# Mixture of experts in a fused kernel: spreading the token weights in groups of four row tiles, and scaling a quarter of the blocks on ScalarE and GpSimd

## The chip, the cores and the metric

The kernel runs on one core of a Trainium2 chip. The metric is the device time of one execution in microseconds (us). The kernel before took 2416.99 us, the median of three runs (2410.0 to 2425.56).

## What is computed

An image of 256x256 positions with 64 channels goes through two convolution-like blocks, a recurrent scan and, last, a mixture of experts. Only the last stage is touched by the change:

```python
def _L1_ffn_ref(x, router_w, router_b, expert_w, expert_b):
    B, N, D, C, E, K = (8, 4096, 64, 64, 8, 2)
    router_probs = jax.nn.softmax(x @ router_w + router_b, axis=-1)
    top_p, top_i = jax.lax.top_k(router_probs, K)
    top_p = top_p / jnp.sum(top_p, axis=-1, keepdims=True)
    expert_out = jnp.einsum('bnd,edc->bnec', x, expert_w) + expert_b
    gathered = jnp.take_along_axis(expert_out, top_i[..., None], axis=2)
    return jnp.einsum('bnk,bnkc->bnc', top_p, gathered)
...
x = _from_tokens(t, x)              # t = tokens of x; the layer norm of t goes into the experts
x = x + _from_tokens(_L1_ffn_ref(_ln_t(t), ...), x)
```

Each token gets the sum of its two best experts, weighed by a softmax over these two. The kernel does it densely: it multiplies the token by its weight for each of the eight experts (six of them are zero) and adds all eight products.

## The kernel before

The stage is the function `experts` (from L1354). Its work is cut into 64 units of 4 rows of the image: 8 token tiles of 128 (H = 2 halves of a row, R = 4 rows). The stage is a software pipeline written out by hand: every engine runs its own list `step(s)` for s from -12 to 65 (L1478, L1567, L1648, L1727, L1827), and each part of a step works on another unit, s + 10, s + 8, s, s - 1 and so on. 48 of the steps, from s = 2, are the body of a loop of eight; the others are written out. Within an engine the order is the program's; between engines there are semaphores. Where a part depends on s modulo 4 it is called a turn below: the routing is done for four units at a time.

What a step does, with the names used later:

- VectorE: `measure(s + 10)` takes the layer norm's statistics (L1495, L1499). `choose` ranks the experts, in four parts, two in turn 0 and two in turn 1. `split_shares` (L1540, turn 3) cuts the weights into two float16 parts. `scale_inputs(s, ...)` (L1551) writes xe, the token block times its weight for each expert: 8 blocks of 128x512 in a unit, each one instruction that reads one PSUM bank of weights. `finish(s - 2)` (L1562) adds the residual.
- GpSimd: `find_scales(s + 10)` (L1603, L1606, L1608) finds the norm's scale after `measure`; `weigh` has four parts, the last of which (turn 2, L1638 to L1643) makes the weights `shares`.
- ScalarE: `take(s + 8)` (L1685) copies the turned tokens out of PSUM, `normalise(s + 9)` (L1674) is eight small activations, `store(s - 2)` issues a DMA, `weigh(s + 2)` (turn 2, L1702, L1703) makes two sigmoids for the experts' shares, `take_outputs(s - 1)` (L1719) copies the experts' sum out of PSUM, `take_logits(s + 8)` (L1693) the router's. `take_shares` (L1711) comes first in turn 3.
- TensorE: `flip(s + 8)` (L1752) is four transposes, `rate(s + 8)` (L1765) the router's matmuls, `turn_shares` (L1775, turn 3) four transposes, `turn_outputs(s - 1)` (L1822) four transposes. `add_experts(s - 1, half)` (L1810) is eight matmuls of 512 columns that add the experts into po, in two halves. `spread_out(u, p)` (L1793) brings the weights of a token tile from 32 rows of wt16 to all 128 partitions, with a 0/1 matrix `select`. It uses a 32-row strip of TensorE for each, and p is 0 to 3.

The part p of `spread_out` fills two of the four PSUM banks pb with eight matmuls from two row strips, p and p + 1. Even parts use banks 0 and 1, odd parts 2 and 3, and VectorE works on one pair while TensorE fills the other: a wait for `xe_dve` at 2p - 2 blocks guards it (L1787). `add_experts(u, 0)` waits for all eight blocks of its unit (L1803).

Of the kernel before, what the change touches and what calls it, by code (L numbers as in the profile page):

```python
# [21 lines left out]
P = 128  # L22
# [1331 lines left out]
def experts(nc, tag, x, packed, selector, out, ident, numbers):  # L1354
# [4 lines left out]
    with Scope(nc, tag) as m:  # L1359
# [11 lines left out]
        xn = [m.sb(f"xn{q}", [P, R, H, C]) for q in range(2)]  # L1371
        xt = [m.sb(f"xt{q}", [P, R * P]) for q in range(4)]
        xd = [m.sb(f"xd{q}", [P, H, R * P]) for q in range(8)]
        xe = [m.sb(f"xe{q}", [P, EP, H, R * P]) for q in range(2)]
        yt = m.sb("yt", [P, R * P])
        stats = [m.sb(f"stats{q}", [P, T, 3]) for q in range(2)]
# [23 lines left out]
        with nc.Block() as block:  # L1400
# [26 lines left out]
            m.sem(n) for n in ("counted", "var_made", "scaled", "multiplied", "known", "xn_made", "xt_made", "zt_made", "l_made", "l_copied"))  # L1427
        ranked, weighed, share_made, w_made, w_turned, w_copied, w_split = (
            m.sem(n) for n in ("ranked", "weighed", "share_made", "w_made", "w_turned", "w_copied", "w_split"))
        spread_a, spread_b, xe_dve = (  # L1430
            m.sem(n) for n in ("spread_a", "spread_b", "xe_dve"))
        e_made, y_copied, y_turned, out_made, seen = (
            m.sem(n) for n in ("e_made", "y_copied", "y_turned", "out_made", "seen"))
        RANK_STEPS, WEIGH_STEPS = 8, 6
        DVE_BLOCKS = 8
        FIRST, LAST, HEAD, TAIL = -12, G + 1, 14, 16

        def run(eng, step):
# [8 lines left out]
        with nc.Block() as block:  # L1447

            @block.sync
            def _(sp):  # L1450
                def load(u):
                    if not u.real:
                        return
                    if (u - 4).real:
                        sp.wait_ge(xn_made, u.n - 3)
                    sp.dma_start(xs[u.mod(4)][:], x[:, :, row_block(u), :]).then_inc(x_in[u.mod(4)], 16)

                def load_rest(u):
                    if not u.real:
                        return  # L1460
                    if (u - 4).real:
                        sp.wait_ge(stored[u.mod(4)], u.div(4) * 16)
                    sp.dma_start(rest[u.mod(4)][:], x[:, :, row_block(u), :]).then_inc(rest_in[u.mod(4)], 16)

                def double(u):
                    if not u.real:
                        return
                    sp.wait_ge(zt_made, u.n + 1)
                    if (u - 8).real:
                        sp.sem_inc(seen, 1)  # L1470
                        sp.wait_ge(xe_dve, (u.n - 7) * DVE_BLOCKS)
                        sp.sem_inc(seen, 1)
# [12 lines left out]
            @block.vector  # L1485
            def _(dve):
# [55 lines left out]
                def scale_inputs(u, p, h):  # L1542
                    if not u.real:
                        return
                    i = (p + h) % R
                    if p == 0 and h == 0:
# [3 lines left out]
                    dve.wait_ge(spread_b if h else spread_a, u.n * R + p + 1)  # L1550
                    dve.tensor_tensor(xe[u.mod(2)][:, :, h, i * P:(i + 1) * P],  # L1551
                                      pb[2 * (p % 2) + h][:].rearrange("p (e t) -> p e t", e=EP),
                                      xd[u.mod(8)][:, h, i * P:(i + 1) * P].unsqueeze(1).to_broadcast([P, EP, P]),
                                      ALU.mult).then_inc(xe_dve, 1)

# [11 lines left out]
                def step(s):  # L1567
                    turn = s.mod(4)
                    four = s + 4 - turn
                    scale_inputs(s, 0, 0)  # L1570
                    scale_inputs(s, 0, 1)
                    finish(s - 2)
                    scale_inputs(s, 1, 0)
                    scale_inputs(s, 1, 1)
                    measure(s + 10)
                    if turn == 0:
                        choose(four, 0)
                    if turn == 1:
                        choose(four, 2)
                    if turn == 3:  # L1580
                        split_shares(s + 1)
                    scale_inputs(s, 2, 0)
                    scale_inputs(s, 2, 1)
                    scale_inputs(s, 3, 0)
                    scale_inputs(s, 3, 1)
                    if turn == 0:
                        choose(four, 1)
                    if turn == 1:
                        choose(four, 3)
# [4 lines left out]
            def _(pool):  # L1594
# [50 lines left out]
                def twofold(t):  # L1645
                    return t[:].rearrange("p (q h) e -> p q (h e)", h=H).unsqueeze(2).to_broadcast([P, 4 * R, 2, H * E])

                def step(s):  # L1648
                    turn = s.mod(4)
                    four = s + 4 - turn  # L1650
                    if turn == 1:
                        weigh(four, 1)
                    find_scales(s + 10)
                    if turn == 0:
                        weigh(four, 0)
                    if turn == 1:
                        weigh(four, 2)
                    if turn == 2:
                        weigh(four, 3)
                run(pool, step)  # L1660

            @block.scalar
            def _(act):
# [23 lines left out]
                def take_logits(u):  # L1687
# [3 lines left out]
                    if (u - 8).real:  # L1691
                        act.wait_ge(w_made, u.div(4) - 1)
                    act.activation(logit[(u.base // 4) % 2][:, u.mod(4), :], rt[:, 0:T * E], ACT.Copy  # L1693
                                   ).then_inc(l_copied, 1)

                def weigh(u):
# [29 lines left out]

                def step(s):  # L1727
                    turn = s.mod(4)
                    if turn == 3:
                        take_shares(s + 1)  # L1730
                    take(s + 8)
                    normalise(s + 9)
                    store(s - 2)
# [10 lines left out]
            def _(pe):  # L1744
# [34 lines left out]
                def spread_out(u, p):  # L1779

                    if not u.real:
                        return
                    if p == 0:
                        pe.wait_ge(w_split, u.div(4) + 1)
                        pe.sem_inc(seen, 1)
                    if p >= 2 or (u - 1).real:
                        pe.wait_ge(xe_dve, u.n * DVE_BLOCKS + 2 * p - 2)  # L1787
                        pe.sem_inc(seen, 1)
                    rows = wt16[(u.base // 4) % 2][:, u.mod(4) * P:(u.mod(4) + 1) * P]
                    for e in range(EP):  # L1790
                        for h in range(H):
                            q = (p + h) % R
                            ins = pe.matmul(pb[2 * (p % 2) + h][:, e * P:(e + 1) * P],  # L1793
                                            select[32 * q:32 * q + 32, h, e, :], rows[32 * q:32 * q + 32, :],
                                            start=True, stop=True)
                            if e == EP - 1:
                                ins.then_inc(spread_b if h else spread_a, 1)

                def add_experts(u, half):
                    if not u.real:  # L1800
                        return
                    if half == 0:
                        pe.wait_ge(xe_dve, (u.n + 1) * DVE_BLOCKS)  # L1803
                        pe.sem_inc(seen, 1)
# [22 lines left out]
                def step(s):  # L1827
                    if s.mod(4) == 3:
                        turn_shares(s + 1)
                    spread_out(s, 2)  # L1830
                    flip(s + 8)
                    add_experts(s - 1, 0)
                    spread_out(s, 3)
                    add_experts(s - 1, 1)
                    spread_out(s + 1, 0)
                    rate(s + 8)
                    spread_out(s + 1, 1)
                    turn_outputs(s - 1)

                run(pe, step)  # L1840

# [108 lines left out]
```

## Time and profile before

| | us |
|---|---|
| median of 3 runs | 2416.99 |
| the profiled execution | 2419.92 |
| its span | 2418.2 |
| the experts' stage, from its first matmuls to the end | about 1846 to 2418 |
| of it the even part, in which every step has all its parts | about 1895 to 2345 |

The span is the time from the first instruction to the last in the profile; the profiled execution is 2.9 us above the median. All engines work in the experts' stage at once, so the time of a step (one of 64 units) is what counts: it is the distance at which a part comes again.

### The profile page before, as it was taken

Reading aid. Unit: us, or ns where it says so; the run is one execution under the profiler, and the core shown is the slowest. Engines: PE = TensorE matmul, PEld = TensorE weight load, DVE = VectorE, ACT = ScalarE, POOL = GpSimd, SP = SyncE. Lnnn points to the kernel's source line nnn. Section 1 sums busy time; section 2 is a strip of 40 time slices with the busy share of each in tenths; the row PEclk is TensorE's granted clock in tenths of the full one; section 3 lists DMA queues with packets and bytes.
Section 4 is the critical chain, followed back from the end, with each engine's and each line's share of the span. In section 5 each row is a group of like instructions: output and inputs, shape, how many; then the busy total and the mean of one; then the engine's idle time right before and its main releaser. Section 6 shows DMA issues by size and latency. Waiting matters only on the chain. (4 is left out here: it accounts for less than half of the span.)

```text
span 2418.2 us, 46313 instructions
## 1 busy us (share of the span) xinstructions
PE 1806.8 (75%) x11740; PEld 1177.9 (49%) x11740; DVE 1522.4 (63%) x4493; ACT 1138.0 (47%) x2610; POOL 1296.9 (54%) x1722
## 2 busy tenths in 40 slices
PE   5777737787746659747777764777864899999998
PEld 2444426777622238624333334777853444444443
DVE  5666512665757768736555640455673788988887
ACT  5778723333215549725555561333314555555541
POOL 6989912776857740036767660466684434433430
PEclk9999979999879989968999987999976799998999
DMA  3656545887743314956777754778864555555552
GB/s 113 184 150 182 160 110 178 292 283 256 235 136 93 94 52 90 190 162 203 219 207 216 228 150 124 231 263 281 263 200 150 152 153 159 160 151 155 156 145 74
DMA packets 508245, 423.17 MB, mean 175 GB/s; under 512 B 224690, under 2 KB 437938, under 8 KB 508082
## 3 DMA queue, kind: packets, MB, share of 16 engines
q1 hardware_dynamic: 435378, 303.87, 45.0%
q10 hardware_dynamic: 72704, 117.47, 14.3%
q8 instruction: 61, 1.00, 0.2%
q14 instruction: 102, 0.84, 0.1%
HBM read 236.68 MB, written 150.99 MB: 160 GB/s over the span
## 5 line engine op out<-in xcount | busy, mean ns | idle before, releaser
L712 PE MATMUL cp_pv<-cp_weight,cp_zt 64*128 64x320 f32 x2048 | 402.5, 493 | 144.5 <-DVE cp_b_stage L530 107.6
L843 PE MATMUL cc_sum<-a_res,cc_bch 128*128 (+1 forms) x2048 | 307.0, 299 | 89.4 <-DMA cc_bch<-b_scratch 87.7
L257 POOL TENSOR_TENSOR cc_ln_rstd<-cc_ln_var,numbers 128x8 f32<-128x8 f32 x128 | 258.2, 2018 | 202.5 <-DVE cc_ln_var L248 192.4
L528 DVE TENSOR_TENSOR a_res<-cp_pv,cp_sig 128x128 f32 (+1 forms) x512 | 191.6, 374 | 266.8 <-ACT cp_sig L659 256.8
L1551 DVE TENSOR_TENSOR ex_xe<-ex_spread,ex_xd 128x512 f32<-128x512 f32 x512 | 322.6, 681 | 36.4 <-PE ex_spread L1793 35.9
L659 ACT ACTIVATE cp_sig<-cp_pv 128x384 f32<-128x384 f32 x512 | 244.7, 491 | 199.9 <-DMA gate_scratch<-cp_sig 135.5
L843 PEld LDWEIGHTS cc_sum<-a_res,cc_bch 128*128 128x128 f32 x2048 | 273.8, 206 | 116.2 <-issue 102.7
L712 PEld LDWEIGHTS cp_pv<-cp_weight,cp_zt 64*128 64x128 f32 x2048 | 186.6, 197 | 291.1 <-issue 270.7
L933 ACT ACTIVATE cc_p<-cc_sum 128x512 f32 (+1 forms) x128 | 135.5, 1058 | 403.6 <-PE cc_sum L843 349.3
L1810 PE MATMUL ex_po<-ex_xe,ex_expert 128*64 128x512 f32 x1024 | 267.6, 646 | 0.3
L1603 POOL TENSOR_TENSOR ex_rstd<-ex_var,numbers 128x8 f32<-128x8 f32 x64 | 104.7, 1636 | 273.5 <-DVE ex_var L1499 268.1
L911 POOL TENSOR_TENSOR cc_p<-cc_p,cc_g 128x512 f32 (+1 forms) x128 | 161.9, 1265 | 130.0 <-DVE cc_g L892 114.3
L639 ACT ACTIVATE cp_xn<-cp_x,cp_lift,cp_rstd 128x64 f32<-128x64 f32 x512 | 196.7, 440 | 67.2 <-POOL cp_lift L579 67.1
L892 DVE TENSOR_TENSOR cc_g<-cc_po,cc_g 128x512 f32<-128x512 f32 x128 | 88.2, 689 | 181.2 <-PE cc_po L861 165.6
L242 DVE BATCH_NORM_STATS2 cc_ln_stats<-cc_p 128x6 f32 (+1 forms) x512 | 111.9, 281 | 141.4 <-ACT cc_p L933 141.2
L1674 ACT ACTIVATE ex_xn<-ex_x,ex_lift,ex_rstd 128x64 f32<-128x64 f32 x512 | 175.8, 428 | 20.9 <-POOL ex_lift L1608 20.9
L604 POOL TENSOR_TENSOR a_res<-a_res,cp_mask 128x512 f32<-128x512 f32 (+1 forms) x128 | 133.4, 1042 | 93.5 <-DVE cp_b_stage L530 92.0
L257 POOL TENSOR_TENSOR si_ln_rstd<-si_ln_var,numbers 128x8 f32<-128x8 f32 x64 | 127.9, 1998 | 68.0 <-DVE si_ln_var L248 68.0
L861 PEld LDWEIGHTS cc_po<-cc_weight,cc_pt 128*128 128x128 f32 x1024 | 150.0, 211 | 5.6
L613 POOL TENSOR_TENSOR cp_b_stage<-cp_b_stage,cp_mask 128x256 f32<-128x256 f32 x256 | 151.4, 613 | 0.0
L861 PE MATMUL cc_po<-cc_weight,cc_pt 128*128 128x128 f32 x1024 | 149.8, 294 | 0.0
L938 ACT ACTIVATE cc_pt<-cc_tp 128x512 f32<-128x512 f32 x128 | 77.6, 606 | 140.1 <-PE cc_tp L851 128.8
(187 smaller groups left out, 3154.0 us busy)
## 6 DMA issues: line engine op xcount, KB each, us to landing
cc_bch<-b_scratch SPq DMA_DIRECT2D x256, 256.0 KB, 4.3
gate_scratch<-cp_sig SPq DMA_DIRECT2D x128, 256.0 KB, 3.0
b_scratch<-cp_b_stage SPq DMA_DIRECT2D x128, 256.0 KB, 3.8
cc_g<-gate_scratch ACTq DMA_DIRECT2D x128, 256.0 KB, 4.1
after_conv<-cc_p ACTq DMA_DIRECT2D x128, 256.0 KB, 3.6
ex_xd<-ex_xt SPq DMA_DIRECT2D x256, 128.0 KB, 2.5
cp_x<-in_x SPq DMA_DIRECT2D x64, 256.0 KB, 3.1
cc_p<-in_x ACTq DMA_DIRECT2D x64, 256.0 KB, 3.2
```

The costliest lines, as they stand in the source:

```text
L257: pool.tensor_tensor(rstd[q][:], var[q][:], numbers[:, 0:1].to_broadcast([P, tiles]), ALU.pow).then_inc(scaled if shifts else known, 1)
L528: dve.tensor_tensor(a_res[:, :, :, bass.ds(row, 1)].rearrange("p h c i -> p h (c i)"), bank[:, :, 3 * C:4 * C], sig[u.mod(2)][:, 0, :, i, ...
L613: ins = pool.tensor_tensor(at, at, over(mask_sb[:, h, row_block(u)], CH).unsqueeze(1) .to_broadcast([P, CHUNKS, R, CH]), ALU.mult)
L639: ins = act.activation(xn[u.mod(2)][:, i, 0, :], xs[u.mod(8)][:, 0, i, :], ACT.Identity, scale=rstd[q][:, k, i * H:i * H + 1], bias=lift[q ...
L659: act.activation(sig[u.mod(2)][:, :, :, i, :].rearrange("p k h c -> p h k c"), pv[slot(u, i)][:, :, 0:3 * C].rearrange("p h (k c) -> p h k ...
L712: pe.matmul(pv[slot(u, i)][:, h, 0:COLS], zt[u.mod(2)][half, i * P:(i + 1) * P], weight[half, :], start=True, stop=True).then_inc(v_made, 1)
L843: ins = pe.matmul(psum[q][:, at:at + TI], bch[buf][:, k, :, c], a_res[:, k, bass.ds(s * SC + j * CH + c, 1), ih * TI:(ih + 1) * TI], start ...
L861: ins = pe.matmul(po[q][:, j * 2 * C:(j + 1) * 2 * C], pt[:, j * P:(j + 1) * P], weight[:], start=False, stop=True, skip_group_check=True)
L911: pool.tensor_tensor(at, at, gs[q][:], ALU.add).then_inc(added, 1)
L1551: dve.tensor_tensor(xe[u.mod(2)][:, :, h, i * P:(i + 1) * P], pb[2 * (p % 2) + h][:].rearrange("p (e t) -> p e t", e=EP), xd[u.mod(8)][:, ...
L1674: ins = act.activation(xn[q][:, i, h, :], xs[u.mod(4)][:, h, i, :], ACT.Identity, scale=rstd[q][:, t:t + 1], bias=lift[q][:, t:t + 1])
L1810: ins = pe.matmul(po[h * HALF:(h + 1) * HALF, :], expert[:, e, :], xe[u.mod(2)][:, e, h, :], start=e == 0, stop=e == EP - 1)
```

## The change

Six things are changed, all in `experts`.

1. The weights are spread in two groups of a unit, g = 0 and 1, in place of four parts. A group is 16 matmuls from all four row strips, one strip to each of the four banks.
2. A group may start only when VectorE has scaled the three blocks of the group before it and ScalarE has copied its fourth.
3. VectorE scales three of the four blocks of a group (6 of 8 in a unit).
4. ScalarE copies the fourth bank to a new buffer xw in SBUF (`take_spread`), once as the first thing of its step, and once behind `normalise`.
5. GpSimd multiplies this copy into xe (a new `scale_inputs`), once ahead of `find_scales` and once as the last thing of its step.
6. TensorE's step is put in another order, and `add_experts(u, 0)` and SyncE's `double` wait for GpSimd's two blocks as well.

```diff
+        xw = [m.sb(f"xw{q}", [P, EP, P]) for q in range(2)]
...
+        DVE_BLOCKS, POOL_BLOCKS = 6, 2
+        FOURS = [[(0, 0), (1, 1), (0, 2), (1, 3)], [(1, 0), (0, 1), (1, 2), (0, 3)]]
...
 # sync, double(u)
                         sp.wait_ge(xe_dve, (u.n - 7) * DVE_BLOCKS)
+                        sp.wait_ge(xe_pool, (u.n - 7) * POOL_BLOCKS)
...
 # vector, scale_inputs(u, g, k)
+                    dve.wait_ge(spread_made[k], u.n * 2 + g + 1)
                     dve.tensor_tensor(xe[u.mod(2)][:, :, h, i * P:(i + 1) * P],
+                                      pb[k][:].rearrange("p (e t) -> p e t", e=EP),
...
 # vector, step(s)
-                    scale_inputs(s, 0, 0)
-                    scale_inputs(s, 0, 1)
+                    for k in range(3):
+                        scale_inputs(s, 0, k)
                     finish(s - 2)
-                    scale_inputs(s, 1, 0)
-                    scale_inputs(s, 1, 1)
                     measure(s + 10)
...
-                    scale_inputs(s, 2, 0)
-                    scale_inputs(s, 2, 1)
-                    scale_inputs(s, 3, 0)
-                    scale_inputs(s, 3, 1)
+                    for k in range(3):
+                        scale_inputs(s, 1, k)
...
 # gpsimd
+                def scale_inputs(u, g):
+                    h, i = FOURS[g][3]
+                    pool.wait_ge(xw_made, u.n * POOL_BLOCKS + g + 1)
+                    pool.tensor_tensor(xe[u.mod(2)][:, :, h, i * P:(i + 1) * P], xw[g][:],
+                                       xd[u.mod(8)][:, h, i * P:(i + 1) * P].unsqueeze(1).to_broadcast([P, EP, P]),
+                                       ALU.mult).then_inc(xe_pool, 1)
...
 # scalar
+                def take_spread(u, g):
+                    act.wait_ge(spread_made[3], u.n * 2 + g + 1)
+                    if (u - 1).real:
+                        act.wait_ge(xe_pool, u.n * POOL_BLOCKS + g - 1)
+                    act.activation(xw[g][:].rearrange("p e t -> p (e t)"), pb[3][:], ACT.Copy).then_inc(xw_made, 1)
...
 # tensor, spread_out(u, g)
-                    if p >= 2 or (u - 1).real:
-                        pe.wait_ge(xe_dve, u.n * DVE_BLOCKS + 2 * p - 2)
+                    if g or (u - 1).real:
+                        pe.wait_ge(xe_dve, u.n * DVE_BLOCKS + g * 3)
+                        pe.wait_ge(xw_made, u.n * POOL_BLOCKS + g)
...
 # tensor, add_experts(u, 0)
                         pe.wait_ge(xe_dve, (u.n + 1) * DVE_BLOCKS)
+                        pe.wait_ge(xe_pool, (u.n + 1) * POOL_BLOCKS)
```

The order of three engines in the loop is shown below; in these lists a line number is that of the kernel the list belongs to. TensorE before, one step in the even part (ex_po is `add_experts`, ex_tp `flip`, ex_routing `rate`, ex_tb `turn_outputs`, ex_spread `spread_out`):

```order
L1793 MATMUL ex_spread<-ex_wt,ex_select 128x128 x8
L1752 MATMUL ex_tp<-ident,ex_xn 128x128 x4
L1810 MATMUL ex_po<-ex_xe,ex_expert 64x512 x4
L1793 MATMUL ex_spread<-ex_wt,ex_select 128x128 x8
L1810 MATMUL ex_po<-ex_xe,ex_expert 64x512 x4
L1793 MATMUL ex_spread<-ex_wt,ex_select 128x128 x8
L1765 MATMUL ex_routing<-ex_router,ex_xt 128x16 x4
L1793 MATMUL ex_spread<-ex_wt,ex_select 128x128 x8
L1822 MATMUL ex_tb<-ident,ex_yt 128x128 x4
```

And TensorE now, one step, with the start of the next:

```order
L1838 MATMUL ex_po<-ex_xe,ex_expert 64x512 x4
L1778 MATMUL ex_tp<-ident,ex_xn 128x128 x4
L1820 MATMUL ex_spread<-ex_wt,ex_select 128x128 x16
L1838 MATMUL ex_po<-ex_xe,ex_expert 64x512 x4
L1791 MATMUL ex_routing<-ex_router,ex_xt 128x16 x4
L1850 MATMUL ex_tb<-ident,ex_yt 128x128 x4
L1820 MATMUL ex_spread<-ex_wt,ex_select 128x128 x16
L1838 MATMUL ex_po<-ex_xe,ex_expert 64x512 x4
```

The transposes ex_tp (`flip`) stood ahead of the first half of ex_po and now stand behind it; the four parts of the spread have become two.

ScalarE now, one step in turn 2 (ex_xt is `take`, ex_xn `normalise`, ex_share the two sigmoids, ex_yt `take_outputs`, ex_logit `take_logits`):

```order
L1718 ACTIVATE ex_xw<-ex_spread 128x512
L1701 ACTIVATE ex_xt<-ex_tp 128x512
L1690 ACTIVATE ex_xn<-ex_x,ex_lift,ex_rstd 128x64 x8
L1718 ACTIVATE ex_xw<-ex_spread 128x512
L1749 DMA out<-ex_rest 256x1x256
L1726 ACTIVATE ex_share<-ex_gap 128x32
L1727 ACTIVATE ex_share<-ex_gap 128x32
L1743 ACTIVATE ex_yt<-ex_po 128x512
L1709 ACTIVATE ex_logit<-ex_routing 128x64
```

The two rows ex_xw are new, and the rest stands as before. GpSimd now, the same step (ex_rstd and ex_lift are `find_scales`, the next three `weigh`'s last part):

```order
L1657 TENSOR_TENSOR ex_xe<-ex_xw,ex_xd 128x4x128
L1603 TENSOR_TENSOR ex_rstd<-ex_var,numbers 128x8
L1606 TENSOR_TENSOR ex_lift<-ex_stats,ex_rstd 128x8
L1608 TENSOR_TENSOR ex_lift<-numbers,ex_lift 128x8
L1638 TENSOR_TENSOR ex_first<-ex_first,ex_share 128x256
L1639 TENSOR_TENSOR ex_second<-ex_second,ex_share 128x256
L1643 TENSOR_TENSOR ex_shares<-ex_first,ex_second 128x512
L1657 TENSOR_TENSOR ex_xe<-ex_xw,ex_xd 128x4x128
```

The first and the last row are new; between them is what GpSimd did in this step before.

## Rows read from the trace of the kernel before

**Rows 1.** Windows: busy us (x instructions) of PE, PEld, DVE, ACT, POOL; clock.

```profile
1895.00:2345.00 450.00, 422.17 (x3465) 210.06 (x3466) 394.39 (x865) 230.18 (x631) 174.86 (x251) 0.93 0.55 154
2345.00:2412.00 67.00, 60.13 (x522) 25.95 (x518) 54.96 (x94) 9.38 (x21) 7.67 (x10) 1.00 0.30 88
```

**Rows 2.** Waits, 1895 to 2345 us: us in total, times, longest us.

```profile
ACT ex_xt L1685 <- PE ex_tp L1752: 102.1, 54, 3.6
ACT ex_yt L1719 <- PE ex_po L1810: 60.6, 53, 3.2
DVE ex_xe L1551 <- PE ex_spread L1793: 27.6, 37, 1.6
PE ex_spread L1793 <- DVE ex_xe L1551: 21.7, 19, 1.3
```

**Rows 3.** Groups by line and shape, 2000 to 2200 us.

```profile
L1551 DVE TENSOR_TENSOR ex_xe<-ex_spread,ex_xd 128x512 f32<-128x512 f32 x192 | 121.1, 681 | 11.8 <-PE ex_spread L1793 11.7
```

**Rows 4.** Timeline of TensorE: one step without a wait.

```profile
2047.80 0.40 PE L1793 MATMUL ex_spread<-ex_wt,ex_select 32*128 32x128 f16 x8
2048.12 0.65 PE L1752 MATMUL ex_tp<-ident,ex_xn 128*128 128x128 f32 x4
2048.71 1.94 PE L1810 MATMUL ex_po<-ex_xe,ex_expert 128*64 128x512 f32 x8
2050.58 0.40 PE L1793 MATMUL ex_spread<-ex_wt,ex_select 32*128 32x128 f16 x8
...
2055.01 0.40 PE L1793 MATMUL ex_spread<-ex_wt,ex_select 32*128 32x128 f16 x8
```

**Rows 5.** Timeline, two steps from `flip` to ScalarE's part, then GpSimd's `weigh`.

```profile
2063.92 0.66 PE L1752 MATMUL ex_tp<-ident,ex_xn 128*128 128x128 f32 x4
...
2064.61 0.60 ACT L1685 ACTIVATE ex_xt<-ex_tp 128x512 f32<-128x512 f32 x1 [2.97 <-PE ex_tp L1752]
...
2073.08 0.43 ACT L1674 ACTIVATE ex_xn<-ex_x,ex_lift,ex_rstd 128x64 f32<-128x64 f32 x1
...
2075.73 0.22 ACT L1702 ACTIVATE ex_share<-ex_gap 128x32 f32<-128x32 f32 x1
2075.85 0.22 ACT L1703 ACTIVATE ex_share<-ex_gap 128x32 f32<-128x32 f32 x1
...
2076.45 0.63 POOL L1638 TENSOR_TENSOR ex_first<-ex_first,ex_share 128x256 f32<-128x256 f32 x1
...
2077.74 1.27 POOL L1643 TENSOR_TENSOR ex_shares<-ex_first,ex_second 128x512 f32<-128x512 f32 x1
```

**Rows 6.** GpSimd's product of two SBUF tiles of 128x512, another stage.

```profile
L911 POOL TENSOR_TENSOR cc_p<-cc_p,cc_g 128x512 f32 x96 | 121.4, 1265 | 83.9 <-DVE cc_g L892 73.6 <-DMA cc_p<-after_scan 6.7 <-DMA cc_p<-in_x 3.4
```

**Rows 7.** Timeline of TensorE: a step with a wait, then the clock falls.

```profile
2096.66 0.61 PE L1793 MATMUL ex_spread<-ex_wt,ex_select 32*128 32x128 f16 x8 [1.29 <-DVE ex_xe L1551]
2097.20 1.12 PE L1752 MATMUL ex_tp<-ident,ex_xn 128*128 128x128 f32 x4
2098.25 2.77 PE L1810 MATMUL ex_po<-ex_xe,ex_expert 128*64 128x512 f32 x8
2100.95 0.40 PE L1793 MATMUL ex_spread<-ex_wt,ex_select 32*128 32x128 f16 x8
```

**Rows 8.** Windows of TensorE: us, busy, granted clock; after two waits, and before the even part.

```profile
2097.00:2098.00 1.00, 1.00 (x10) 0.50 0.63 141
2061.00:2064.00 3.00, 1.71 (x25) 1.00 0.84 225
1846.00:1896.00 50.00, 33.35 (x176) 0.50 0.56 163
```

**Rows 9.** Timeline of TensorE and ScalarE in the last steps.

```profile
2374.85 0.62 PE L1793 MATMUL ex_spread<-ex_wt,ex_select 32*128 32x128 f16 x16
...
2377.27 1.94 PE L1810 MATMUL ex_po<-ex_xe,ex_expert 128*64 128x512 f32 x8
...
2383.83 1.51 PE L1810 MATMUL ex_po<-ex_xe,ex_expert 128*64 128x512 f32 x6
```

More of the change, by code:

```diff
@@ L1429, in experts @@
             m.sem(n) for n in ("ranked", "weighed", "share_made", "w_made", "w_turned", "w_copied", "w_split"))
-        spread_a, spread_b, xe_dve = (
-            m.sem(n) for n in ("spread_a", "spread_b", "xe_dve"))
+        spread_made = [m.sem(f"spread_made{q}") for q in range(4)]
+        xw_made, xe_dve, xe_pool = (m.sem(n) for n in ("xw_made", "xe_dve", "xe_pool"))
         e_made, y_copied, y_turned, out_made, seen = (
@@ L1434, in experts @@
         RANK_STEPS, WEIGH_STEPS = 8, 6
-        DVE_BLOCKS = 8
+        DVE_BLOCKS, POOL_BLOCKS = 6, 2
+        FOURS = [[(0, 0), (1, 1), (0, 2), (1, 3)], [(1, 0), (0, 1), (1, 2), (0, 3)]]
         FIRST, LAST, HEAD, TAIL = -12, G + 1, 14, 16
@@ L1471, in double @@
                         sp.wait_ge(xe_dve, (u.n - 7) * DVE_BLOCKS)
+                        sp.sem_inc(seen, 1)
+                        sp.wait_ge(xe_pool, (u.n - 7) * POOL_BLOCKS)
                         sp.sem_inc(seen, 1)
@@ L1540, in split_shares, with scale_inputs @@
                     dve.tensor_tensor(wt16[(u.base // 4) % 2][:], rt[:], low16[:], ALU.subtract).then_inc(w_split, 1)
-                def scale_inputs(u, p, h):
+                def scale_inputs(u, g, k):
                     if not u.real:
                         return
-                    i = (p + h) % R
-                    if p == 0 and h == 0:
+                    h, i = FOURS[g][k]
+                    if g == 0 and k == 0:
                         dve.wait_ge(doubled[u.mod(8)], u.div(8) * (16 * H * 2) + 16 * H * 2)
@@ L1549, in scale_inputs @@
                             dve.wait_ge(e_made, (u.n - 1) * H)
-                    dve.wait_ge(spread_b if h else spread_a, u.n * R + p + 1)
+                    dve.wait_ge(spread_made[k], u.n * 2 + g + 1)
                     dve.tensor_tensor(xe[u.mod(2)][:, :, h, i * P:(i + 1) * P],
-                                      pb[2 * (p % 2) + h][:].rearrange("p (e t) -> p e t", e=EP),
+                                      pb[k][:].rearrange("p (e t) -> p e t", e=EP),
                                       xd[u.mod(8)][:, h, i * P:(i + 1) * P].unsqueeze(1).to_broadcast([P, EP, P]),
@@ L1646, in twofold @@
                     return t[:].rearrange("p (q h) e -> p q (h e)", h=H).unsqueeze(2).to_broadcast([P, 4 * R, 2, H * E])
+                def scale_inputs(u, g):
+                    if not u.real:
+                        return
+                    h, i = FOURS[g][3]
+                    if g == 0:
+                        pool.wait_ge(doubled[u.mod(8)], u.div(8) * (16 * H * 2) + 16 * H * 2)
+                        if (u - 2).real:
+                            pool.wait_ge(e_made, (u.n - 1) * H)
+                    pool.wait_ge(xw_made, u.n * POOL_BLOCKS + g + 1)
+                    pool.tensor_tensor(xe[u.mod(2)][:, :, h, i * P:(i + 1) * P], xw[g][:],
+                                       xd[u.mod(8)][:, h, i * P:(i + 1) * P].unsqueeze(1).to_broadcast([P, EP, P]),
+                                       ALU.mult).then_inc(xe_pool, 1)
                 def step(s):
@@ L1652, in step @@
                         weigh(four, 1)
+                    scale_inputs(s, 0)
                     find_scales(s + 10)
@@ L1659, in step @@
                         weigh(four, 3)
+                    scale_inputs(s, 1)
                 run(pool, step)
@@ L1694, in take_logits @@
                                    ).then_inc(l_copied, 1)
+                def take_spread(u, g):
+                    if not u.real:
+                        return
+                    act.wait_ge(spread_made[3], u.n * 2 + g + 1)
+                    if (u - 1).real:
+                        act.wait_ge(xe_pool, u.n * POOL_BLOCKS + g - 1)
+                    act.activation(xw[g][:].rearrange("p e t -> p (e t)"), pb[3][:], ACT.Copy).then_inc(xw_made, 1)
                 def weigh(u):
@@ L1728, in step @@
                     turn = s.mod(4)
+                    take_spread(s, 0)
                     if turn == 3:
@@ L1732, in step @@
                     normalise(s + 9)
+                    take_spread(s, 1)
                     store(s - 2)
@@ L1777, in turn_shares, with spread_out @@
                     ins.then_inc(w_turned, 1)
-                def spread_out(u, p):
+                def spread_out(u, g):
                     if not u.real:
                         return
-                    if p == 0:
+                    if g == 0:
                         pe.wait_ge(w_split, u.div(4) + 1)
                         pe.sem_inc(seen, 1)
-                    if p >= 2 or (u - 1).real:
-                        pe.wait_ge(xe_dve, u.n * DVE_BLOCKS + 2 * p - 2)
+                    if g or (u - 1).real:
+                        pe.wait_ge(xe_dve, u.n * DVE_BLOCKS + g * 3)
+                        pe.sem_inc(seen, 1)
+                        pe.wait_ge(xw_made, u.n * POOL_BLOCKS + g)
                         pe.sem_inc(seen, 1)
@@ L1790, in spread_out @@
                     for e in range(EP):
[L1791 to L1795, printed above, removed]
+                        for k, (h, i) in enumerate(FOURS[g]):
+                            ins = pe.matmul(pb[k][:, e * P:(e + 1) * P], select[32 * i:32 * i + 32, h, e, :],
+                                            rows[32 * i:32 * i + 32, :], start=True, stop=True)
                             if e == EP - 1:
-                                ins.then_inc(spread_b if h else spread_a, 1)
+                                ins.then_inc(spread_made[k], 1)
                 def add_experts(u, half):
@@ L1803, in add_experts @@
                         pe.wait_ge(xe_dve, (u.n + 1) * DVE_BLOCKS)
+                        pe.sem_inc(seen, 1)
+                        pe.wait_ge(xe_pool, (u.n + 1) * POOL_BLOCKS)
                         pe.sem_inc(seen, 1)
@@ L1829, in step @@
                         turn_shares(s + 1)
-                    spread_out(s, 2)
+                    add_experts(s - 1, 0)
                     flip(s + 8)
-                    add_experts(s - 1, 0)
-                    spread_out(s, 3)
+                    spread_out(s, 1)
                     add_experts(s - 1, 1)
+                    rate(s + 8)
+                    turn_outputs(s - 1)
                     spread_out(s + 1, 0)
-                    rate(s + 8)
-                    spread_out(s + 1, 1)
-                    turn_outputs(s - 1)
                 run(pe, step)
```

## The prediction

> **What bounds the kernel now.** Only the experts' stage changes, so I first cut the span into windows. In its even part [rows 1] TensorE is busy for 422.2 of 450 us and VectorE for 394.4, ScalarE for 230.2 and GpSimd for 174.9. ScalarE's copy of the turned tokens comes 54 times there [rows 2], so a step takes 450/54 = 8.33 us. The last 67 us have hardly any norm or routing work. The list of waits [rows 2] then says who holds whom: TensorE waits for VectorE's blocks 19 times (21.7 us), VectorE for TensorE's spread 37 times (27.6 us). Two nearly full engines in one loop pay for both. The timeline of TensorE gives the step it could have: in rows 4 a spread starts at 2047.80 and the same one of the next step at 2055.01, 7.21 us. With the four transposes of the shares in every fourth step (0.6/4) that is 7.36. The other 0.97 us are waits and stretches at the lower clock.
>
> The clock is the second thing to see. After a wait of 1.29 us the granted clock was 0.50 (1.2 of 2.4 GHz), and eight matmuls of the experts' sum took 2.77 in place of 1.94 [rows 7, 8]. After another wait of the same length it stayed at 1.00 [rows 8]. In the timeline from 2006 to 2175 us, 21 steps, I counted 11 waits of TensorE of 0.68 to 1.30 us (the one of rows 7 among them); 6 were followed by such a dip, each costing about 1.5 us (in rows 7: spread 0.21, transposes 0.46, sum 0.83).
>
> **The change part by part, at full clock.**
>
> VectorE loses 2 of 8 blocks. The 192 such blocks from 2000 to 2200 us kept it busy for 121.1 us [rows 3], so one costs 0.63 (a record is 681 ns, the start of the next lies under it). It gains 1.26 us a step, against 394.4/54 = 7.30 busy. TensorE's four spreads cost 0.33 each (2050.58 to 2050.91, where the next sum starts) = 1.30. Two groups of 16 cost 0.33 each if the four strips run together, 0.66 if they run as two pairs do. The saving is 0 to 0.65, and TensorE's own step 6.6 to 7.2. So by the two old bounds a step could fall to about 7.2. This is what the change offers; what it adds is a new loop.
>
> Call T the moment at which `add_experts(s - 1, 0)` starts. It now waits for GpSimd's second block of unit s - 1. In step s:
>
> - the half takes 1.87 (2048.71 to 2050.58 [rows 4]); only then come `flip`'s transposes, which stood ahead of it: T + 1.87.
> - ScalarE's `take` starts 0.69 after them (2063.92 to 2064.61 [rows 5]): T + 2.56.
> - `normalise` starts 0.50 later, and its eight activations hold ScalarE for 2.65 (2073.08 to 2075.73 [rows 5]): T + 5.71. Behind them in the queue stands the second `take_spread`, though its bank was filled at about T + 2.9.
> - the copy of 128x512 takes 0.60, as `take`'s does: T + 6.31. GpSimd's block is not in the trace before. Its nearest row is the product of two SBUF tiles of this size, 1.265 [rows 6]; 1.27 for L1643 of the same output [rows 5] agrees. I take 1.27. A handoff is short: the transposes end at 2064.58 and ScalarE's copy starts at 2064.61 [rows 5]. With 0.06 for each of two, the next `add_experts` starts at T + 7.70.
> - the other branch: `take_outputs` starts 0.50 behind the copy, ends at T + 6.81, TensorE turns the outputs from T + 6.87 to T + 7.46 (0.59) and then spreads, 0.33 to 0.66, before the next half: T + 7.79 to T + 8.12. I take 7.96.
>
> So three of four steps cannot be shorter than 7.96, whatever VectorE saves. VectorE's 7.30 less 1.26 fits into it.
>
> Turn 2 is worse. GpSimd's second block stands behind `weigh`'s last part, and that waits for the two sigmoids, which now stand behind the second copy: T + 5.71 + 0.50 + 0.34 (2075.73 to 2076.07) = T + 6.55. `weigh` takes 2.56 (2076.45 to 2079.01 [rows 5]): T + 9.17. Then 1.27 and handoffs: T + 10.5. In the old kernel nothing on TensorE's path but the routing's own transposes waited for this part. VectorE and TensorE find nothing to do meanwhile except those transposes.
>
> Four steps: 3 x 7.96 + 10.5 = 34.4, a mean of 8.60, which is 0.27 above the 8.33 measured now, and the 8.33 holds its dips already.
>
> **The clock on top.** In every step TensorE is out of work from about T + 5.8 to T + 6.9 (1.1 us) and again for some tenths, and in turn 2 for over 2 us. Before, such waits came in 11 of 21 steps, and half of them brought a dip. A dip begins behind the wait, where now the turned outputs, the spread, the half and the transposes follow, and these 3.4 us are all in the loop. With a dip in half of the steps at 1.5 us, 0.75 a step is added: 9.35. Ends: nothing (8.60) and a dip in every step (10.1). Rows 8 show the far end: before the even part, TensorE was busy for 33 of 50 us with short waits between small groups, at 0.50 throughout.
>
> The Trainium skill (TensorE: Matmul & The Clock Gate, "A second HAM failure mode: psum-queue depth-cycling") says that brief pauses between groups while cycling through PSUM banks can make the clock swing between its two levels. Rows 7 agree for one wait and rows 8 disagree for another. By that rule alone every step would dip, 10.1; by rows 8 alone none, 8.60. For the spread, TensorEngine Tiling (Array Packing), "Key Properties", of the Trainium skill says that tiles of different row strips load and multiply in parallel; a group of 16 would then take what 8 take now. Rows 9 have 16 from overlapping strips in 0.62, which does not show it for four distinct ones. By the rule the branch is 7.79, by the row 8.12.
>
> **The last steps.** Without norm and routing, ScalarE is free. A step is now 2383.83 - 2377.27 = 6.56 [rows 9]. In the new order: half 1.87, spread about 0.5, half 1.87, then the copy of the outputs 0.1 + 0.6 + 0.1, turn 0.59, spread 0.5 = 6.1 or a little less; GpSimd's block is ready by T + 4.4. That is some 0.5 saved in each of 9 or 10 steps, 5 us.
>
> **Sum.** 54 x (9.35 - 8.33) = 55, minus 5: +50 on the profiled execution of 2419.9, or 2417 + 50 = 2467 on the median, which is 2.9 lower. DMA is no term: its busy share is 0.55 [rows 1]; xe and xd have as many buffers as before, and SyncE's `double` waits for blocks that are needed seven steps later.
>
> **Rivals.** A measurement tells about 1% (24 us) from no change.
>
> 1. The loop holds, and the clock does not dip in it: 54 x 0.27 - 5 = +10, 2427. For it: five of eleven waits brought no dip, and the loop leaves TensorE slack for the second half and `rate`. Against it: the waits come in every step. Chance 0.20.
> 2. A dip in nearly every step: 54 x 1.77 - 5 = +91, 2508. For it: the window at 0.50 [rows 8]. Against it: that window had none of the experts' large matmuls. Chance 0.16.
> 3. The other side: the loop through ScalarE is not tight, because `flip` and the copies run ahead of where I put them, and the relief of VectorE is what counts. The step would be TensorE's 6.9 + 0.15 with the old dips of 0.45, 7.5: 54 x -0.83 - 5 = -50, 2367. It decides once the second copy starts about 1 us earlier and turn 2's GpSimd block no longer waits for `weigh`. Against it: all these orders are fixed in the program, and each of the durations in the loop has a row. Chance 0.07.
> 4. The four strips do not run together: a group costs 0.66, a step at most 0.16 more than I took; this is within the forecast's own range.
>
> The forecast itself has 0.57, with a range of 2440 to 2490. The 80% range reaches into rivals 1 and 2: 2426 to 2500. Slower by over 1% (2441 and more): 0.57 x 0.96 + 0.16 + 0.02 of rival 1 = 0.73. Faster by over 1%: 0.06. The rest, 0.21, is within 1%.
>
> **What would show it.** Right: in the even part ScalarE's xt copies come about every 9.3 us; TensorE's wait ahead of ex_tb is released by ScalarE's ex_yt and that ahead of ex_po by GpSimd's ex_xe; turn 2 is the longest step by some 2.5 us; GpSimd's block lasts 1.27; the granted clock of the stage is below 0.93; VectorE's busy share falls to 6.1/9.3, near 65%. Wrong: steps near 7.5 with a full TensorE, or ex_xw starting before the eight activations end. If the clock stays at 0.93 or above and steps are 8.6, rival 1 was right; at 0.75 and 10, rival 2.

## The result, and the profile after

The changed kernel took 2483.35 us (median of 4 runs, 2476.94 to 2489.04), against 2413.49 us of the kernel before (4 runs): a ratio of 1.0281, 95% interval 1.0233 to 1.0330. That is 70 us slower; 50 were forecast.

The windows of the changed kernel, with the columns of [rows 1]:

```profile
1895.00:2345.00 450.00, 372.36 (x2927) 172.65 (x2929) 284.64 (x639) 231.55 (x619) 262.54 (x304) 0.84 0.49 131
2430.00:2470.00 40.00, 32.66 (x322) 12.36 (x318) 29.15 (x49) 11.79 (x21) 19.60 (x18) 1.00 0.26 80
```

VectorE fell from 394.4 us busy to 284.6, and TensorE from 422.2 to 372.4, but in fewer steps. The granted clock fell from 0.93 to 0.84. ScalarE's copy of the turned tokens shows the length of a step:

```profile
L1701 ACT ACTIVATE ex_xt<-ex_tp 128x512 f32<-128x512 f32 x45 | 26.9, 597 | 149.3 <-PE ex_tp L1778 149.3
```

45 copies in 450 us are 10.0 us a step, against 54 and 8.33. Per step VectorE is busy for 6.3 us in place of 7.3, which is what the change is for; TensorE is busy for 8.3 in place of 7.8, although it has no more work to do, because more of it runs at half clock. The waits of 1950 to 2400 us (us in total, times, longest) answer to [rows 2]:

```profile
ACT ex_xt L1701 <- PE ex_tp L1778: 150.2, 45, 4.5
DVE ex_xe L1555 <- PE ex_spread L1820: 149.1, 64, 3.8
POOL ex_xe L1657 <- ACT ex_xw L1718: 101.4, 51, 5.4
...
PE ex_tb L1850 <- ACT ex_yt L1743: 53.2, 45, 1.5
...
PE ex_po L1838 <- POOL ex_xe L1657: 5.5, 16, 0.4
```

VectorE now waits for TensorE, TensorE in every one of 45 steps for ScalarE's copy of the outputs (ex_yt), and GpSimd for ScalarE's copy of the spread (ex_xw). These waits lead to ScalarE, an engine that is busy half of the time, and ScalarE itself waits for TensorE's `flip` (ex_tp) in every step: the loop is closed. The timeline shows the loop in one step at full clock (TensorE, then ScalarE and GpSimd):

```profile
2024.60 1.94 PE L1838 MATMUL ex_po<-ex_xe,ex_expert 128*64 128x512 f32 x8
2026.47 0.66 PE L1778 MATMUL ex_tp<-ident,ex_xn 128*128 128x128 f32 x4
2027.06 0.40 PE L1820 MATMUL ex_spread<-ex_wt,ex_select 32*128 32x128 f16 x16
2027.40 1.94 PE L1838 MATMUL ex_po<-ex_xe,ex_expert 128*64 128x512 f32 x8
2029.26 1.06 PE L1791 MATMUL ex_routing<-ex_router,ex_xt 128*128 128x16 f32 x8
2031.42 0.65 PE L1850 MATMUL ex_tb<-ident,ex_yt 128*128 128x128 f32 x4 [1.10 <-ACT ex_yt L1743]
...
2032.79 3.17 PE L1838 MATMUL ex_po<-ex_xe,ex_expert 128*64 128x512 f32 x8 [0.32 <-POOL ex_xe L1657]
```

```profile
2030.31 0.58 ACT L1718 ACTIVATE ex_xw<-ex_spread 128x512 f32<-128x512 f32 x1
2030.79 0.58 ACT L1743 ACTIVATE ex_yt<-ex_po 128x512 f32<-128x512 f32 x1
2030.97 1.52 POOL L1657 TENSOR_TENSOR ex_xe<-ex_xw,ex_xd 128x512 f32<-128x512 f32 x1
```

With T = 2024.60 the second copy starts at T + 5.71, as worked out, and TensorE's outputs at T + 6.82 (6.87). The bank of that copy was filled at 2027.46, 2.9 us before. The next half starts at T + 8.19; it follows one long wait, and it runs at half clock (3.17 us for what took 1.94).

The whole time tells less than the stage does. The stages before the experts hold the same instructions in every kernel here, and yet the first statistics of the experts began between 1815.0 and 1839.5 us in twelve profiles; in this pair at 1839.5 (before) and 1820.3 (after). So I also compare the stage: from the start of the first ex_xt copy to the end of the span it took 2418.2 - 1846.9 = 571.3 us before and 2483.6 - 1827.7 = 655.9 after, 84.6 more. That is one execution of each; the medians of four say 70, with the interval of the ratio 56 to 80.

### The profile page after: what moved, and what is told of

Same layout as the page of the kernel before. It is cut to its first block and busy times, and to the rows that moved or that the text cites. A ratio compares the mean times of both kernels' runs of the same rounds, so it can differ in the third digit from the quotient of the medians.

```text
span 2483.6 us, 46919 instructions
## 1 busy us (share of the span) xinstructions
PE 1799.4 (72%) x11740; PEld 1153.1 (46%) x11740; DVE 1455.3 (59%) x4365; ACT 1195.1 (48%) x2738; POOL 1459.0 (59%) x1850
## 5 line engine op out<-in xcount | busy, mean ns | idle before, releaser
L712 PE MATMUL cp_pv<-cp_weight,cp_zt 64*128 64x320 f32 x2048 | 395.2, 486 | 141.7 <-DVE cp_b_stage L530 104.0
L1555 DVE TENSOR_TENSOR ex_xe<-ex_spread,ex_xd 128x512 f32<-128x512 f32 x384 | 241.2, 683 | 201.4 <-PE ex_spread L1820 200.7
L1838 PE MATMUL ex_po<-ex_xe,ex_expert 128*64 128x512 f32 x1024 | 307.1, 728 | 16.4 <-POOL ex_xe L1657 8.6
L1657 POOL TENSOR_TENSOR ex_xe<-ex_xw,ex_xd 128x512 f32<-128x512 f32 x128 | 163.5, 1282 | 150.9 <-ACT ex_xw L1718 150.5
L861 PEld LDWEIGHTS cc_po<-cc_weight,cc_pt 128*128 128x128 f32 x1024 | 144.5, 204 | 5.2
L861 PE MATMUL cc_po<-cc_weight,cc_pt 128*128 128x128 f32 x1024 | 144.3, 287 | 0.0
```

Of the source, the lines that this page charges most:

```text
L712: pe.matmul(pv[slot(u, i)][:, h, 0:COLS], zt[u.mod(2)][half, i * P:(i + 1) * P], weight[half, :], start=True, stop=True).then_inc(v_made, 1)
L861: ins = pe.matmul(po[q][:, j * 2 * C:(j + 1) * 2 * C], pt[:, j * P:(j + 1) * P], weight[:], start=False, stop=True, skip_group_check=True)
L1657: pool.tensor_tensor(xe[u.mod(2)][:, :, h, i * P:(i + 1) * P], xw[g][:], xd[u.mod(8)][:, h, i * P:(i + 1) * P].unsqueeze(1).to_broadcast([ ...
L1838: ins = pe.matmul(po[h * HALF:(h + 1) * HALF, :], expert[:, e, :], xe[u.mod(2)][:, e, h, :], start=e == 0, stop=e == EP - 1)
```

## The experiments

Each ran in three rounds with the kernel before beside it. "Stage" is that measure, in the one profiled execution.

| kernel | median us | ratio to before, 95% | stage us | clock, 1895 to 2275 us |
|---|---|---|---|---|
| before | 2410 to 2413 | 1 | 571 | 0.92 |
| changed | 2483.4 | 1.028 (1.023 to 1.033) | 656 | 0.84 |
| flip first | 2407.3 | 0.998 (0.995 to 1.000) | 567 | 0.94 |
| copy first | 2495.5 | 1.034 (1.030 to 1.038) | 653 | 0.84 |
| filler | 2447.4 | 1.015 (1.011 to 1.019) | 611 | 0.98 |
| turn 2 | 2450.3 | 1.015 (1.011 to 1.018) | 614 | 0.86 |
| flip first and turn 2 | 2353.9 | 0.976 (0.970 to 0.981) | 518 | 0.99 |
| all on VectorE | 2433.3 | 1.012 (1.005 to 1.018) | 600 | 0.92 |
| three orders | 2344.0 | 0.972 (0.967 to 0.978) | 506 | 0.99 |
| before, flip late | 2464.6 | 1.023 (1.018 to 1.029) | 623 | 0.87 |
| before, routing orders | 2381.9 | 0.989 (0.986 to 0.993) | 551 | 0.94 |
| three orders, all on VectorE | 2363.5 | 0.981 (0.978 to 0.985) | 530 | 1.00 |

A dip is counted below where the first half of `add_experts` took over 2.1 us (1.94 at full clock), from 1900 to 2270 us. There are 12 in 43 steps before, and 24 in 37 in the changed kernel: there the half at the start of turns 1 and 3 dips every time, that of turn 2 in 6 of 9, and that of turn 0 never.

**Flip first.** In TensorE's step of the changed kernel:

```diff
-                    add_experts(s - 1, 0)
                     flip(s + 8)
+                    add_experts(s - 1, 0)
                     spread_out(s, 1)
```

> The changed kernel with one order undone: TensorE's transposes (flip) stand ahead of the first half of the experts' sum again, as before the change. My theory (the loop add_experts, flip, ScalarE's take and normalise, second copy, GpSimd's block, add_experts sets the step): ScalarE starts 1.87 us earlier, so a step outside turn 2 falls from 8.2 (10.1 with a clock dip) to 7.1 to 7.6 us, turn 2 to about 9, and the whole to 2350 to 2400 us. Rival A (the loss is the offload itself: a slow GpSimd block, three engines in place of one): no gain, 2460 to 2490. Rival B (the four banks filled at once leave no bank to work on in the meantime): no gain either, 2460 to 2490.

2407 us: one line takes back the whole loss, 76 us. Both rivals fall: the offload and the four banks are as in the changed kernel. The time is 7 us above my range. Steps outside turn 2 take 7.4 to 8.8, the long one because VectorE's last three operations of turn 0 wait for GpSimd (and for more than a wait, see the last section), and turn 2 takes 9.7, not 9: flip stands behind turn_shares there, and that waits 2.0 us for GpSimd's shares. Dips are down to 12 in 44 steps, nearly all behind this wait. TensorE at the end of one turn 2:

```profile
2035.60 0.66 PE L1801 MATMUL ex_routing<-ident,ex_shares 128*128 128x128 f32 x4 [2.08 <-POOL ex_shares L1643]
2036.09 0.60 PE L1778 MATMUL ex_tp<-ident,ex_xn 128*128 128x128 f32 x4
2037.08 3.58 PE L1838 MATMUL ex_po<-ex_xe,ex_expert 128*64 128x512 f32 x8 [0.38 <-POOL ex_xe L1657]
```

**Copy first.** `take_spread(s, 1)` moved from behind `normalise(s + 9)` to ahead of it, on ScalarE alone.

> The changed kernel with ScalarE's second copy of the spread moved ahead of normalise. My theory has two branches of nearly one length: this shortens GpSimd's, but the copy of the outputs still stands behind all of take, copy and normalise, so TensorE's outputs come no earlier. Steps fall by 0 to 0.3 us, turn 2 not at all: 2465 to 2485 us. Rival (GpSimd's branch alone binds): 1 us or more per step, 2430 or less.

2495 us, no gain, against the rival by 65. GpSimd's branch was shortened, and outside turn 2 TensorE's half no longer waits for it, but the outputs still come at T + 6.8, because take, normalise and both copies are the same sum in any order. Undipped steps of turn 0 fell from 8.2 us to between 7.9 and 8.1, and those of turn 2 stayed at 10.7, as worked out; the mean stayed at 10.0, with 27 dips in 37 steps. The median is 10 us above my range and 12 above the changed kernel, but the stage is not longer (653 against 656), and the two intervals overlap.

**Filler.** Six matmuls ahead of the wait for the outputs:

```diff
+                    for i in range(6):
+                        pe.matmul(tb[:, (i % R) * P:(i % R + 1) * P], ident[:], ident[:], start=True, stop=True)
                     pe.wait_ge(y_copied, u.n + 1)
```

> The changed kernel with six needless 128x128 float32 matmuls (identity times identity, overwritten at once) into the bank of the turned outputs, in the wait ahead of turn_outputs: 0.9 us of TensorE work at full clock in a wait of 1.1. If the clock dips cost 1.2 us a step, as the trace suggests, most go: the granted clock of the even part rises from 0.84 to 0.90 or more, a step falls from 10.0 to about 9.2, the whole to 2420 to 2450 us, although TensorE does more. Rival (the dips cost nothing, since the loop has slack for them): 2483 or more. At half clock the filler itself takes 1.8 us and may cost up to 0.7 us in a step that dips all the same.

2447 us, and the clock of the windows is 0.98. TensorE's rows, two steps outside turn 2:

```profile
2043.99 1.94 PE L1838 MATMUL ex_po<-ex_xe,ex_expert 128*64 128x512 f32 x8
2045.86 1.06 PE L1791 MATMUL ex_routing<-ex_router,ex_xt 128*128 128x16 f32 x8
2046.77 1.58 PE L1849 MATMUL ex_tb<-ident 128*128 128x128 f32 x12
2048.19 0.61 PE L1852 MATMUL ex_tb<-ident,ex_yt 128*128 128x128 f32 x4
...
2049.26 1.94 PE L1838 MATMUL ex_po<-ex_xe,ex_expert 128*64 128x512 f32 x8
...
2057.43 1.94 PE L1838 MATMUL ex_po<-ex_xe,ex_expert 128*64 128x512 f32 x8 [0.15 <-issue]
```

Useless work made the kernel 36 us faster: 4 halves in 41 steps dip, in place of 24 in 37. Undipped steps outside turn 2 are now 7.9 to 8.2, except that every second one of turn 1 takes 9.1 to 9.3, for a reason that stays open; turn 2 takes 10.7 to 10.9. The filler is longer than I meant. Each call is two instructions, 1.42 us in all, and the outputs are turned at T + 6.99 in place of 6.82 (2056.25, with T = 2049.26), so up to 0.2 us a step is lost to that. The step's mean is 9.0 (50 copies in 450 us), not the 9.2 that I expected.

**Turn 2.** ScalarE's `weigh(s + 2)` first in its step, and GpSimd's `weigh(four, 3)` ahead of `find_scales`, in turn 2.

> The changed kernel with turn 2 alone put in another order: ScalarE's two sigmoids come first in its step, and GpSimd's last part of weigh comes ahead of find_scales, so that GpSimd's second block no longer waits for either. My theory: turn 2's step falls by 2.5 us (10.7 to 8.2), a quarter of that on the mean, 0.6 x 54 = 34 us, and with fewer dips behind that wait up to 45: 2438 to 2452 us. Rival (turn 2's length is only TensorE's and VectorE's routing work): no gain, 2475 to 2490.

2450 us, at the upper end of the range: 33 us.

**Flip first and turn 2.** Both edits.

> The changed kernel with both orders mended: flip ahead of the first half (as in the run of flip alone, 2407 us, 8.5 us a step with turn 2 at 9.7) and, in turn 2, the sigmoids and weigh's last part ahead of find_scales. My theory: turn 2 falls from 9.7 to about 7.6, 0.53 on the mean, 28 us: 2365 to 2390 us, faster than before the change. Rival (the two mended orders shorten one and the same wait): 2400 to 2412, no gain over flip alone.

2354 us, 11 below my range and 2.4% faster than before the change. The second edit is worth 53 us on top of the first, more than the 33 it gave alone. With no wait of 2 us left, the clock is 0.99, with 2 dips in 49 steps, although 12 waits of 1.0 to 1.2 us remain.

**All on VectorE.** The changed kernel without its offload: three of its blocks in a group become four on VectorE, `take_spread`, GpSimd's `scale_inputs` and their waits go.

> The changed kernel with its groups of 16 and its order on TensorE, but all 8 blocks on VectorE again: no copy to xw, no block on GpSimd. If the loss comes from the loop through the second copy and GpSimd's block, it goes: VectorE is full again with 7.3 us a step and 0.4 to 0.8 us of bare waits for the refilled banks, steps 8.2 to 8.6, 2400 to 2435 us. If it comes from filling all four banks at once (nothing for VectorE to work on while TensorE refills), it stays or grows: 2470 or more.

2433 us, at the upper end of the range for my theory: the long loop through the second copy is gone. 21 us of loss against before remain. The late flip is still in this kernel, and TensorE's turned shares wait up to 1.6 us for GpSimd here, as in the run "before, flip late"; that this is the whole of the 21 us is not shown.

**Three orders.** As flip first and turn 2, and in turn 0 `choose(four, 0)` on VectorE ahead of `measure`, `weigh(four, 0)` on GpSimd ahead of `find_scales`.

> As flip and turn 2 mended, and in turn 0 VectorE's first reduction of choose ahead of measure and GpSimd's first part of weigh ahead of find_scales, so that VectorE's chain of three at the end of turn 0 no longer waits 0.8 us for GpSimd and then delays the next step's blocks (in the run of flip alone the step of turn 1 took 8.8 us against 7.4). My theory: 0.8 to 1.2 us less in one of four steps, 10 to 16 us: 2350 to 2378 us. Rival (that wait is hidden): the same as without it.

2344 us, the fastest. It is 10 us less than without the turn 0 order, the low end of the expected gain; the time is 6 us below my range, which was built on a base that was itself too high.

**Before, flip late.** The kernel before with only the order that the change gave to flip:

```diff
-                    flip(s + 8)
                     add_experts(s - 1, 0)
+                    flip(s + 8)
                     spread_out(s, 3)
```

> The kernel before the change, with only its flip moved behind the first half of the experts' sum, as the change has it. No copy of the spread and no GpSimd block. By the same chain of durations ScalarE's outputs come at T + 6.3 and TensorE's next half could start at T + 7.3, less than the 8.3 a step takes: 2405 to 2440 us. If the late flip is harmful by itself and the offload is innocent: 2460 or more.

2465 us: a clear miss. Three quarters of the change's loss are in this line, without any offload. TensorE, ScalarE and GpSimd of that run around turn 2:

```profile
2051.28 0.21 ACT L1702 ACTIVATE ex_share<-ex_gap 128x32 f32<-128x32 f32 x1
2051.40 0.21 ACT L1703 ACTIVATE ex_share<-ex_gap 128x32 f32<-128x32 f32 x1
2051.69 0.63 POOL L1638 TENSOR_TENSOR ex_first<-ex_first,ex_share 128x256 f32<-128x256 f32 x1 [1.31 <-ACT ex_share L1703]
...
2052.99 1.28 POOL L1643 TENSOR_TENSOR ex_shares<-ex_first,ex_second 128x512 f32<-128x512 f32 x1
2054.32 1.11 PE L1775 MATMUL ex_routing<-ident,ex_shares 128*128 128x128 f32 x4 [1.51 <-POOL ex_shares L1643]
```

I had followed only the outputs, which are in time (that wait is 0.4 us). The sigmoids stand behind the same normalise: T + 5.9 here, with T = 2045.39. GpSimd's shares end at T + 8.9, and TensorE turns them at the head of the next step, where it waited 1.5 us, and at half clock (1.11 for four transposes) afterwards. Before the change this wait was 0.8 at most, 6.2 us in total from 1895 to 2345 us; now it is 18.2. The clock of the whole stretch is 0.87, with 19 dips in 39 steps. That the whole 52 us go this way is read from these rows: no run has the late flip with only the sigmoids moved in the old kernel.

**Before, routing orders.** The kernel before with turn 2 and turn 0 ordered as in the fastest.

> The kernel before the change (all 8 blocks on VectorE, four parts of the spread, flip early) with only the orders of the routing moved as in the fastest run so far: sigmoids and weigh's last part early in turn 2, the first reduction and weigh's first part early in turn 0. If that run (2344 us) is fast because VectorE and TensorE were relieved, this gains little, the two engines still share 7.2 and 7.3 us of work a step: 2390 to 2412 us. If the orders alone carry the gain: 2340 to 2365.

2382 us, between the two: these orders alone gain 28 us of the old kernel.

**Three orders, all on VectorE.**

> The fastest run's orders and its groups of 16, but all 8 blocks on VectorE and none on ScalarE and GpSimd. VectorE then has 7.3 us of work a step and a bare wait of some 0.4 us for the refilled banks, once or twice: steps 7.7 to 8.1, 2375 to 2405 us, if the offload is what gives the gain; 2340 to 2355 if it is the grouping of the spread with the orders.

2364 us, again between, and below the range of the first case. Against the kernel with the routing orders and the old spread (2382) the groups of 16 with TensorE's new order are worth 18 us, and against this one the offload is worth 20 us (2364 to 2344). Orders 28, grouping 18 and offload 20 make up the way from before to the fastest. VectorE is the bound here, 360.0 of 380 us busy, and TensorE waits for it; from 1895 to 2275 us:

```profile
PE ex_spread L1812 <- DVE ex_xe L1553: 47.4, 85, 1.1
```

12 of these waits are 1.0 us or longer, and yet one half in 48 steps dips.

## Why the prediction was right, and where it was off

- **The loop** (T + 5.71, T + 6.31, T + 6.87): right to 0.05 us, in the rows of the changed kernel above. The undipped step was worked out as 7.96 and is 8.19 (2024.60 to 2032.79). What ends it is not the branch that I took for the longer one: the outputs' branch is done at T + 7.79, the low end of mine, and the half waits for GpSimd's block, which I had put at T + 7.70. Its block took 1.52 us in this turn for 1.27, and 0.30 more passed until TensorE went on, for 0.06. So 7.96 came close because the two branches are nearly equal, in part by luck. 8.19 is the step of turn 0, the only one outside turn 2 that was ever undipped; in the filler run turn 3 took 7.95.
- **Turn 2** at 10.5: an undipped one took 10.70 (2083.49 to 2094.19), and turn 2 mended alone gives 33 us.
- **The spread's group of 16** at 0.33 or 0.66: 0.34 (2027.06 to 2027.40), for 16 matmuls, against 0.33 for 8 before. Four row strips do run together. The rule of the Trainium skill (TensorEngine Tiling (Array Packing), "Key Properties") held, and the trace agrees; my 0.5 was between the two.
- **The clock** is the term that was mis-sized. "With a dip in half of the steps at 1.5 us, 0.75 a step": from 2002 to 2115 us, 8 of 12 steps dip, and (3 x 8.19 + 10.70)/4 = 8.82 against the measured 10.0 leaves 1.18 a step, or 1.8 for a dip. So dips were both more frequent (0.65 a step) and dearer than I took; in each the half ran 3.1 to 3.7 us, against 2.77 in rows 7. Why a dip cost less in the old kernel is not shown. By filler, 36 us of this is shown on the chip. The rule on pauses between groups (the Trainium skill, TensorE: Matmul & The Clock Gate, "A second HAM failure mode: psum-queue depth-cycling") points the right way and does not say how often: no run dips in every step; the most are 29 in 39, in the run of turn 2 alone.
- **The last steps**: after the last ex_xt copy 68.2 us before, 65.0 now; 3 saved, not 5.
- **The sum**: in the stage the steps cost 87.8 (first to last of the 64 ex_xt copies: 503.1 before, 590.9 after) and the rest gives back 3.2. Of these 84.6 the whole shows 65 in the profiled pair and 70 in the medians, as the stages ahead of it vary. Against this pair the forecast of 50 is low by the clock's 0.43 a step (23 us) and 0.22 of the undipped step (12 us). Steps of 10.0 us are those of rival 2 (10.1), whose time was 2508. That the median of 2483 lies in my range of 2440 to 2490 owes something to luck: my own sum with steps of 10.0 gives 2502. The clock of 0.84 lies between rival 1's 0.93 and rival 2's 0.75.
- **Rival 3** (the relief of VectorE counts, 2367) named what decides: the second copy 1 us earlier and turn 2's block not behind weigh. These two edits gave 2354.

What my account did not see is which part of the change does it. I named the loop with its offload; in the old kernel the same late flip alone costs 52 us, of the change's 70, and the rows show it going through the sigmoids. Flip late and the offload are not two sums: without flip late the offload with its groups costs nothing (2407), with it 19 us more (2465 to 2483).

It stays open how much of a dip's cost each stretch of the loop takes: no run held the clock down or up without changing something else.

## What to carry to other kernels

When engines that are half idle get new work, write down the chain through them once round a step, with the start of each instruction and not its busy time; the order in each queue decides, and moving one group of transposes by two microseconds was worth more than the quarter of VectorE's blocks. An order is only right for a given set of waits: after an offload, look again at what stands ahead of the instruction that releases another engine. And a wait on TensorE costs more than its length when the clock falls behind it, so a stall that seems hidden can be worth removing, or filling; count the dips in the trace first, for not every wait brings one.

## What the runs showed of the hardware

**VectorE is held up by GpSimd's block.** The same operation of VectorE on 128x256 with two inputs in SBUF takes 425 ns in the kernel before and in the run with three orders and all on VectorE. With GpSimd's block it takes this (groups of VectorE from 1950 to 2250 us; count, busy us, mean ns). First the changed kernel:

```profile
L1528 DVE TENSOR_TENSOR ex_first<-ex_work,ex_pick 128x256 f32<-128x256 f32 x8 | 7.4, 921 | 0.3
```

Flip first, in two lines of the turn:

```profile
L1524 DVE SCALAR_TENSOR_TENSOR ex_work<-ex_below,ex_pack 128x256 f32<-128x256 f32 x9 | 13.2, 1471 | 7.1 <-POOL ex_below L1622 7.1
L1538 DVE TENSOR_TENSOR ex_second<-ex_work,ex_pick 128x256 f32<-128x256 f32 x9 | 9.2, 1022 | 0.3
```

Three orders:

```profile
L1528 DVE TENSOR_TENSOR ex_first<-ex_work,ex_pick 128x256 f32<-128x256 f32 x10 | 13.6, 1355 | 0.3
```

Three orders with all on VectorE, where GpSimd has no block of its own:

```profile
L1526 DVE TENSOR_TENSOR ex_first<-ex_work,ex_pick 128x256 f32<-128x256 f32 x10 | 4.3, 425 | 0.3
```

The timeline of three orders shows one of them beside GpSimd's block:

```profile
2056.57 1.27 POOL L1657 TENSOR_TENSOR ex_xe<-ex_xw,ex_xd 128x512 f32<-128x512 f32 x1
2056.76 1.35 DVE L1528 TENSOR_TENSOR ex_first<-ex_work,ex_pick 128x256 f32<-128x256 f32 x1
```

GpSimd ends at 2057.84 and VectorE 0.27 later: it stood still nearly until the other was done. It goes the other way too: GpSimd's block of 1.52 us in the changed kernel (2030.97) began while a VectorE operation of this kind was running (2030.93, 0.43). VectorE's blocks ex_xe, which read one input from PSUM, stay at 680 to 683 ns in all kernels. The Trainium skill has this (SBUF — State Buffer, "SBUF: two separate sides"): a VectorE operation with two SBUF inputs and a GpSimd operation that reads SBUF take one shared port pair in turns, for a whole instruction. The rows agree. It costs up to 1 us once or twice in four steps: by the rows above 0.12 us a step of VectorE's time in the changed kernel, and 0.41 in flip first, (1471 - 426 + 1022 - 425)/4.

**TensorE's clock fell behind waits of about 1 us in some kernels and not in others**: behind 6 of 11 waits before, in 24 of 37 steps in the changed kernel, in 4 of 41 with the filler (clock 0.98). In "flip first and turn 2" and in "three orders, all on VectorE" there were 12 waits of 1.0 us or more each, and 2 and 1 dips in 49 and 48 steps (0.99 and 1.00). So a wait's length does not decide it by itself; what else does stays open. Work that the result does not need made the kernel faster.
